# A relational graph layer: every second adjacency chunk is loaded in quadrant form and turned by VectorE

## The chip, the cores and the metric

The kernel runs on one core of a Trainium2 chip. The metric is the device time of one execution in microseconds. The core has TensorE (PE), VectorE (DVE), ScalarE (ACT), GpSimd (POOL) and SyncE (SP), each with a queue of its own that is worked off in order; SP and ACT can issue DMA transfers from theirs. Waits are on semaphores.

## What is computed

For each of 8 batches there is x (1024 x 128, float32) and an adjacency matrix of 1024 x 1024 int32. Its entries are 0 or, as drawn here, 1; the kernel checks on the way that nothing else occurs and has a second, general path for that case, which does not run with these inputs.

```python
masks = (relation[None] == rel_ids[:, None, None, None]).astype(x.dtype)   # rel_ids 1..4
h = jnp.einsum('rbnm,bmd->rbnd', masks, x)
y = jnp.einsum('rbnd,rdo->bno', h, weight) + bias
out = layernorm(x + y)                                                     # over the last axis
```

## The kernel before, in words

**Chunks.** The adjacency of a batch is cut into 4 chunks of 256 rows (1 MB of int32 each), 32 chunks in all, u = 0 to 31. SBUF holds them as 128 partitions of 2048 words, in a ring of 8 slots (`NADJ`). Partition p of chunk c holds rows 8p + 2c and 8p + 2c + 1. A half (`hf`, 0 to 15) is two chunks, so half a batch.

**The way of a chunk.** SP issues the load (`load_adj`, L152). ACT converts the int32 words to fp8 bytes (`convert_chunk`, L171, `mask`, ring of 4). The product needs the columns of the adjacency on the partitions, so PE transposes the mask, four bytes taken together as one float32 word, in four transposes of 128 x 128 words into a PSUM bank (`turn_words`, L178, `tp_ps`). DVE copies that bank to SBUF (`evacuate`, L182, `maskT`, ring of 6) and ORs the words into `seen` (L451), from which the check for other values is made at the end (`find_others`).

**Products.** x is split into three bf16 parts (`x_sb`'s upper halves, `x_rest`'s upper halves, `x_fine`). Each half takes 3 x 8 matmuls of 512 columns (L194) into one bank of `h_ps`; ACT copies the bank (L386), PE multiplies by the weight (`project_half`, L201), DVE adds x + bias (`add_half`, L477), takes mean and variance (L207, L212, L216), POOL makes the scale and the shift, and DVE (L223) and ACT (L398) each normalise half of the rows. Outputs are stored by SP behind all loads.

**Order.** Each engine's program is written out by hand. On PE the half `hf` is

```python
for part in range(PARTS):
    last = part_products(part, b % NX, b % 2, slice(place, place + 2), bank_of(hf))
    if part == 0:
        turn(2 * hf + 2)
    if part == 1:
        project_half(hf - 1)
        turn(2 * hf + 3)
```

and ACT's turn for it is `copy_half(hf)`, `convert(2 * hf + 5)`, `finish_half(hf - 1)`, `convert(2 * hf + 6)`. Chunks 0 and 1 come as four pieces with shorter products; the first and the last half are cut in quarters. SP's queue in the start is: pieces of chunk 0, x of batch 0, pieces of chunk 1, chunks 2 and 3, x 1, chunk 4, bias, weight, chunk 5, x 2, chunks 6 to 9, x 3, and so on; a chunk from 8 on waits until the one eight back is converted.

## Time and profile before

| | us |
|---|---|
| median of 3 runs | 139.17 |
| lowest, highest | 138.47, 139.57 |
| the profiled execution | 138.68 |
| its span in the profile | 136.9 |
| PE busy | 124.1 |
| DVE busy | 85.8 |
| ACT busy | 83.0 |
| POOL busy | 69.2 |
| read from HBM, written | 37.88 MB, 4.19 MB |

The span is what the profile shows between the first and the last instruction; the execution's own time is 1.8 us longer. Busy times are those of one engine added up, and say nothing yet about which one the others wait for.

### The profile page before, as it was taken

What the parts mean: (1) busy time and instruction counts of PE and PEld (TensorE: products, weight loads), DVE (VectorE), ACT (ScalarE), POOL (GpSimd) and SP (SyncE); (2) the same over time, 40 slices, a digit from 0 to 9 for tenths busy, and PEclk for the clock granted to TensorE, in tenths of its full rate; (3) what the DMA queues carried; (4) which work ended last, traced back from release to release, by engine and by line L of the source; (5) the groups of instructions that cost most, each with busy time, mean ns of one, the idle gap of its engine ahead of it and who ended that gap; (6) DMA issues with size and microseconds to landing.
All of it is one profiled execution on the core that took longest, in us unless ns stands there. A gap on an engine that the chain in (4) does not pass through costs nothing.

```text
span 136.9 us, 2235 instructions
## 1 busy us (share of the span) xinstructions
PE 124.1 (91%) x727; PEld 77.2 (56%) x727; DVE 85.8 (63%) x270; ACT 83.0 (61%) x85; POOL 69.2 (51%) x79
## 2 busy tenths in 40 slices
PE   5986799489999999999999999999999999997920
PEld 2355688346564747465565656565656474666810
DVE  1185213765758494958677675757585939488851
ACT  3655753379785848484848586777758484513040
POOL 3000019975295709680786259553957195405440
PEclk9999999999999999999999999999999999999985
DMA  4999969999999999999999999999913000300422
GB/s 125 415 427 418 427 230 419 421 426 414 426 426 406 423 421 421 420 423 417 412 419 424 414 424 424 424 412 414 382 59 158 0 0 0 153 0 0 160 77 84
DMA packets 7789, 42.24 MB, mean 309 GB/s; under 512 B 864, under 2 KB 1376, under 8 KB 3936
## 3 DMA queue, kind: packets, MB, share of 16 engines
q1 hardware_dynamic: 7776, 42.08, 75.3%
q8 instruction: 7, 0.11, 0.3%
q14 instruction: 6, 0.05, 0.1%
HBM read 37.88 MB, written 4.19 MB: 307 GB/s over the span
## 4 chain that ended last, share of the span: by engine, by line
PE 73%; DMA 15%; SPq 4%; ACT 2%; DVE 1%; issue 1%; POOL 1%
PE h_ps L194 54%; DMA adj_sb<-in_adj_dram 15%; PE y_ps L201 10%; PE tp_ps L178 9%; ACT mask L171 1%; SPq L152 1%; SPq L258 1%; SPq L155 1%; POOL scale L219 1%; ACT h_sb L392 0%; DVE out_sb L223 0%; DVE stats L207 0%; ACT out_sb L398 0%; SPq L270 0%; SPq L269 0%
## 5 line engine op out<-in xcount | busy, mean ns | idle before, releaser
L171 ACT ACTIVATE mask<-adj_sb 128x2048 fp8e4<-128x2048 int32 x30 | 57.2, 1906 | 9.0 <-DMA adj_sb<-in_adj_dram 9.0
L194 PE MATMUL h_ps<-maskT,x_sb 128*128 128x512 fp8e4 (+1 forms) x152 | 32.0, 352 | 3.5 <-DVE maskT L182 2.5
L194 PE MATMUL h_ps<-maskT,x_fine 128*128 128x512 fp8e4 (+1 forms) x152 | 32.0, 352 | 0.4 <-DVE x_fine L164 0.4
L194 PE MATMUL h_ps<-maskT,x_rest 128*128 128x512 fp8e4 (+1 forms) x152 | 32.0, 352 | 0.1
L182 DVE COPY maskT<-tp_ps 128x512 uint32<-128x512 uint32 x30 | 20.6, 686 | 17.2 <-PE tp_ps L178 17.2
L167 POOL TENSOR_TENSOR x_bias<-x_sb,bias_sb 128x1024 f32<-128x1024 f32 x8 | 19.0, 2380 | 18.2 <-DMA bias_sb<-in_L_gnn_bias_dram 18.2
L194 PEld LDWEIGHTS h_ps<-maskT,x_sb 128*128 128x128 bf16 x152 | 14.3, 96 | 18.7 <-DVE maskT L182 2.9
L335 POOL TENSOR_SCALAR minus_mean<-mean_var 128x4 f32<-128x4 f32 (+1 forms) x16 | 3.1, 193 | 41.7 <-issue 22.9
L477 DVE TENSOR_TENSOR total<-y_ps,x_bias 128x512 f32<-128x512 f32 (+1 forms) x17 | 11.2, 660 | 20.2 <-issue 19.2
L386 ACT COPY h_sb<-h_ps 128x512 f32<-128x512 f32 x13 | 7.6, 585 | 23.4 <-issue 23.4
L178 PE MATMUL tp_ps<-identity,mask 128*128 128x128 f32 x128 | 21.1, 286 | 0.7 <-ACT mask L171 0.4
L178 PEld LDWEIGHTS tp_ps<-identity,mask 128*128 128x128 f32 x128 | 18.8, 204 | 4.9 <-ACT mask L171 1.2
L194 PEld LDWEIGHTS h_ps<-maskT,x_fine 128*128 128x128 bf16 x152 | 14.7, 97 | 11.8 <-DVE x_fine L164 0.7
L194 PEld LDWEIGHTS h_ps<-maskT,x_rest 128*128 128x128 bf16 x152 | 14.7, 97 | 11.3 <-DVE x_rest L161 0.3
L451 DVE TENSOR_TENSOR seen<-seen,tp_ps 128x512 uint32<-128x512 uint32 x30 | 20.3, 677 | 0.0
L201 PEld LDWEIGHTS y_ps<-w_sb,h_sb 128*128 128x128 f32 x128 | 16.6, 191 | 3.7 <-ACT h_sb L392 1.4
L219 POOL TENSOR_TENSOR scale<-var_eps,power 128x4 f32<-128x4 f32 (+1 forms) x17 | 17.8, 1046 | 1.7 <-DVE var_eps L216 1.7
L201 PE MATMUL y_ps<-w_sb,h_sb 128*128 128x128 f32 x128 | 17.3, 277 | 1.2 <-ACT h_sb L392 1.2
L398 ACT ACTIVATE out_sb<-total,shift,scale 128x128 f32<-128x128 f32 x31 | 13.6, 486 | 7.8 <-POOL shift L340 7.8
L207 DVE BATCH_NORM_STATS2 stats<-total 128x6 f32<-128x128 f32 x64 | 13.9, 279 | 0.2
L164 POOL TENSOR_TENSOR x_fine<-x_rest 128x1024 bf16<-128x1024 f32 x7 | 13.3, 1893 | 0.1
L161 POOL TENSOR_TENSOR x_rest<-x_sb 128x1024 f32<-128x1024 f32 x7 | 13.3, 1895 | 0.0
(28 smaller groups left out, 46.4 us busy)
## 6 DMA issues: line engine op xcount, KB each, us to landing
adj_sb<-in_adj_dram SPq DMA_DIRECT2D x30, 1024.0 KB, 17.6
x_sb<-in_x_dram SPq DMA_DIRECT2D x8, 512.0 KB, 17.9
out_dram<-out_sb SPq DMA_DIRECT2D x7, 512.0 KB, 7.7
adj_sb<-in_adj_dram SPq DMA_DIRECT2D x4, 512.0 KB, 5.2
out_dram<-out_sb SPq DMA_DIRECT2D x1, 256.0 KB, 2.0
out_dram<-out_sb SPq DMA_DIRECT2D x2, 128.0 KB, 1.8
bias_sb<-in_L_gnn_bias_dram SPq DMA_DIRECT2D x1, 64.0 KB, 14.8
w_sb<-in_L_gnn_weight_dram SPq DMA_DIRECT2D x1, 64.0 KB, 14.6
```

The lines of the kernel that those rows point to most:

```text
L161: eng.tensor_tensor(x_rest[:, slot], x_sb[:, x_slot], upper(x_sb[:, x_slot]), ALU.subtract).then_inc(done, 1)
L164: eng.tensor_tensor(x_fine[:, slot], x_rest[:, slot], upper(x_rest[:, slot]), ALU.subtract).then_inc(done, 1)
L167: nc.gpsimd.tensor_tensor(x_bias[:, slot], x_sb[:, x_slot], bias_sb[:, :].unsqueeze(1).to_broadcast([P, TILES, D]), ALU.add).then_inc(done, 1)
L171: nc.scalar.activation(mask[:, slot % NMASK], adj_sb[:, slot % NADJ], ACT.Copy, saturate=False).then_inc(done, 1)
L178: last = nc.tensor.transpose(tp_ps[:, bank, place:place + P], words[:, o, j], identity[:, :])
L182: nc.vector.tensor_copy(maskT[:, place].rearrange("k j o p e -> k (j o p e)").bitcast(u32), tp_ps[:, bank].bitcast(u32)).then_inc(done, 1)
L194: last = nc.tensor.matmul(h_ps[:, bank, 0:n], x_t, m_t, start=(part == 0 and t == 0), stop=(part == PARTS - 1 and t == TILES - 1))
L201: last = nc.tensor.matmul(y[:, n, :], h_of(r)[:, s], w_sb[:, r, :], start=(r == 0), stop=(r == relations - 1))
L207: last = nc.vector.bn_stats(stats[:, slot, s, :], total[:, place, s, :])
L219: nc.gpsimd.tensor_tensor(scale[:, slot, tiles], var_eps[:, slot, tiles], power[:, tiles], ALU.pow).then_inc(done, by)
L398: last = nc.scalar.activation(out_sb[:, b, s, :], total[:, b % NTOTAL, s, :], ACT.Identity, bias=shift[:, b % 2, s:s + 1], scale=scale[:, ...
L451: nc.vector.tensor_tensor(seen[:, :], seen[:, :], tp_ps[:, tp_bank(u)].bitcast(u32), ALU.bitwise_or).then_inc(collected, 1)
```

## The change

Chunks with u > 4 and u odd (5, 7, ..., 31, fourteen of them; `by_blocks`) are no longer loaded by SP. ACT issues them, each as four transfers (`load_quadrant`), at places written into its program: chunk 5 before the conversion of chunk 2, chunk 7 behind it, 9 and 11 behind those of chunks 3 and 4, 13 and 15 behind those of 6 and 8, and then 2 * hf + 13 at the end of the turn for each half. Quadrant q fills partitions 32q to 32q + 31 with the columns 256q to 256q + 255 of the chunk's 256 rows, in 256 runs of 256 words (1 KB). After the conversion, one transposition of 32 x 32 blocks on DVE (`turn_blocks`) brings `maskT` into the form that the product wants; no transpose on PE and no copy from PSUM is made for these chunks, and DVE's OR reads `mask` in place of the bank.

Since the rows of a quadrant are every fourth row, the rows of a chunk are numbered anew for all chunks: partition p of a row-wise chunk c holds rows 8p + c and 8p + 4 + c, two runs of 4 KB in place of one of 8 KB. The projection of a `by_blocks` chunk reads `h_sb` with a stride of two (`rows_of`), and `total` and `out_sb` are addressed through `tile_of` and `by_chunk`. The last batch's stores are cut by chunk (`store_chunks`), in runs of 1 KB and 512 B. The general path's store and sums follow the new order. The core of the diff:

```diff
     NBANK = 3
     NTP = 3
     PIECED = 2
+    Q = 4
+    S = P // Q
     NY = 2
     BANK = 512
     EPS = 1e-5
...
     x_p = x.rearrange("b (p t) d -> b p (t d)", p=P)
     out_p = out.rearrange("b (p t) d -> b p (t d)", p=P)
-    adj_p = adj.rearrange("b (p c o) m -> b c p (o m)", p=P, c=CH)
+    out_t = out.rearrange("b (p o c) d -> b p o (c d)", p=P, c=CH)
+    adj_p = adj.rearrange("b (p o c) m -> b c p o m", p=P, c=CH)
+    adj_q = adj.rearrange("b (g r c) (q m) -> b c q r g m", r=S, c=CH, q=Q)
 
     ctx = ExitStack()
     with ctx:
...
             return values.bitcast(bf16).rearrange("p t (d two) -> p t two d", two=2)[:, :, 1, :]
 
         def load_adj(eng, b, ch, slot, done):
-            eng.dma_start(adj_sb[:, slot], adj_p[b, ch]).then_inc(done, 16)
+            eng.dma_start(adj_sb[:, slot].rearrange("p (o m) -> p o m", o=O), adj_p[b, ch]).then_inc(done, 16)
+
+        def load_quadrant(eng, b, ch, slot, q, done):
+            eng.dma_start(adj_sb[q * S:(q + 1) * S, slot].rearrange("r (g m) -> r g m", m=N // Q),
+                          adj_q[b, ch, q]).then_inc(done, 16)
 
         def load_x(eng, b, slot, done):
             eng.dma_start(flat(x_sb[:, slot]), x_p[b]).then_inc(done, 16)
 
-        def store(eng, b, place, tiles, done):
-            eng.dma_start(out_p[b][:, tiles.start * D:tiles.stop * D], flat(out_sb[:, place, tiles])).then_inc(done, 16)
+        def by_chunk(tiles):
+            return tiles.rearrange("p (o c) d -> p c o d", o=O)
+
+        def tile_of(s):
+            return s // O + CH * (s % O)
+
+        def store(eng, b, place, done):
+            eng.dma_start(out_p[b], flat(out_sb[:, place])).then_inc(done, 16)
+
+        def store_chunks(eng, b, place, chunks, done):
+            eng.dma_start(out_t[b][:, :, chunks.start * D:chunks.stop * D],
+                          out_sb[:, place].rearrange("p (o c) d -> p o (c d)", o=O)[:, :, chunks.start * D:chunks.stop * D]
+                          ).then_inc(done, 16)
 
         def take_rest(eng, x_slot, slot, done):
             eng.tensor_tensor(x_rest[:, slot], x_sb[:, x_slot], upper(x_sb[:, x_slot]), ALU.subtract).then_inc(done, 1)
...
         def evacuate(bank, place, done):
             nc.vector.tensor_copy(maskT[:, place].rearrange("k j o p e -> k (j o p e)").bitcast(u32),
                                   tp_ps[:, bank].bitcast(u32)).then_inc(done, 1)
+
+        def turn_blocks(slot, place, done):
+            blocks = mask[:, slot].bitcast(u32).rearrange("r (g s j) -> r j g s", s=S, j=J)
+            nc.vector.transpose(maskT[:, place].rearrange("k j o p e -> k (j o p e)").bitcast(u32), blocks).then_inc(done, 1)
 
         def evacuate_tile(bank, place, o, done):
             nc.vector.tensor_copy(maskT[:, place, :, o].rearrange("k j p e -> k j (p e)").bitcast(u32),
...
                                         start=(part == 0 and t == 0), stop=(part == PARTS - 1 and t == TILES - 1))
             return last
 
-        def project(h_of, y, relations, tiles, done, by):
-            for n, s in enumerate(range(tiles.start, tiles.stop)):
-                for r in range(relations):
-                    last = nc.tensor.matmul(y[:, n, :], h_of(r)[:, s], w_sb[:, r, :],
-                                            start=(r == 0), stop=(r == relations - 1))
-            last.then_inc(done, by)
+        def project(rows, y, r, relations, n):
+            return nc.tensor.matmul(y[:, n, :], rows, w_sb[:, r, :], start=(r == 0), stop=(r == relations - 1))
+
+        def rows_of(h, u, c, o):
+            if by_blocks(u):
+                return h[:, c * O:(c + 1) * O].rearrange("d t p -> d (t p)").rearrange("d (p o) -> d o p", o=O)[:, o]
+            return h[:, c * O + o]
 
         def measure_rows(slot, place, tiles, done, by):
             for s in range(tiles.start, tiles.stop):
-                last = nc.vector.bn_stats(stats[:, slot, s, :], total[:, place, s, :])
+                last = nc.vector.bn_stats(stats[:, slot, s, :], total[:, place, tile_of(s), :])
             last.then_inc(done, by)
 
         def aggregate_rows(slot, tiles, done, by):
...
         def normalize(b, slot, place, tiles, done, by):
             for s in tiles:
-                last = nc.vector.tensor_scalar(out_sb[:, b, s, :], total[:, place, s, :], mean_var[:, slot, s, 0:1],
-                                               scale[:, slot, s:s + 1], ALU.subtract, ALU.mult)
+                last = nc.vector.tensor_scalar(out_sb[:, b, tile_of(s), :], total[:, place, tile_of(s), :],
+                                               mean_var[:, slot, s, 0:1], scale[:, slot, s:s + 1], ALU.subtract, ALU.mult)
             last.then_inc(done, by)
 
         def bank_of(hf, c=0):
             return (hf + 2 if hf > 1 else 2 * hf) % NBANK if c == 0 else (bank_of(hf) + c) % NBANK
 
+        def by_blocks(u):
+            return u > CH and u % 2 == 1
+
+        def by_rows_before(u):
+            return sum(not by_blocks(v) for v in range(PIECED, u))
+
         def tp_bank(u, o=0):
-            return (PIECED * O + u - PIECED if u >= PIECED else O * u + o) % NTP
+            return (PIECED * O + by_rows_before(u) if u >= PIECED else O * u + o) % NTP
+
+        def last_in_bank(u):
+            turned_before = PIECED * O + by_rows_before(u) - NTP
+            if turned_before < PIECED * O:
+                return turned_before // O
+            return [v for v in range(PIECED, u) if not by_blocks(v)][turned_before - PIECED * O]
+
+        def landed(u):
+            return sum(16 * (Q if by_blocks(v) else 1) for v in range(PIECED, u + 1) if v % NADJ == u % NADJ)
 
         def gathered(u):
             return u + 1 + PIECED * (O - 1) if u >= PIECED else O * u + 1
...
                 load_x(sp, b, b % NX, x_loaded[b % NX])
 
             def load_piece(u, o):
-                sp.dma_start(adj_sb[:, u, o * N:(o + 1) * N],
-                             adj_p[0, u][:, o * N:(o + 1) * N]).then_inc(piece_loaded[O * u + o], 16)
+                sp.dma_start(adj_sb[:, u, o * N:(o + 1) * N], adj_p[0, u][:, o]).then_inc(piece_loaded[O * u + o], 16)
 
             load_piece(0, 0)
             load_piece(0, 1)
...
             for b in range(LAST):
                 sp.wait_ge(normed, CH * (b + 1))
                 sp.wait_ge(act_normed, CH * (b + 1))
-                store(sp, b, b, ALL, stored)
+                store(sp, b, b, stored)
             sp.wait_ge(normed, CH * LAST + 2)
             sp.wait_ge(act_normed, CH * LAST + 2)
-            store(sp, LAST, LAST, HALF[0], stored)
+            store_chunks(sp, LAST, LAST, slice(0, 2), stored)
             for c in range(2):
                 sp.wait_ge(normed, CH * LAST + 3 + c)
                 sp.wait_ge(act_normed, CH * LAST + 3)
-                store(sp, LAST, LAST, QUARTER[2 + c], stored)
+                store_chunks(sp, LAST, LAST, slice(2 + c, 3 + c), stored)
 
             sp.wait_ge(flag_ready, 1)
             again = sp.value_load(flag[0:1, 0:1], min_val=0, max_val=P)
...
         @block.scalar
         def _(act):
             def convert(u):
-                act.wait_ge(adj_loaded[u % NADJ], 16 * (u // NADJ + (1 if u % NADJ >= PIECED else 0)))
+                act.wait_ge(adj_loaded[u % NADJ], landed(u))
                 if u >= NMASK:
-                    wait_chunk(act, piece_turned, turned, u - NMASK)
+                    free_mask(u - NMASK)
                 convert_chunk(u, masked)
+
+            def free_mask(u):
+                if by_blocks(u):
+                    act.wait_ge(evacuated, u - PIECED + 1)
+                    act.wait_ge(collected, gathered(u) + 1)
+                elif u >= PIECED:
+                    act.wait_ge(turned, by_rows_before(u) + 1)
+                else:
+                    act.wait_ge(piece_turned, O * (u + 1))
+
+            def load_blocks(u):
+                if u >= NADJ:
+                    wait_chunk(act, piece_masked, masked, u - NADJ)
+                for q in (0, 2, 1, 3):
+                    load_quadrant(act, u // CH, u % CH, u % NADJ, q, adj_loaded[u % NADJ])
 
             def copy_half(hf):
                 act.wait_ge(multiplied, 2 * (hf + 1))
...
                     act.wait_ge(piece_loaded[O * u + o], 16)
                     nc.scalar.activation(mask[:, u, o * N:(o + 1) * N], adj_sb[:, u, o * N:(o + 1) * N],
                                          ACT.Copy, saturate=False).then_inc(piece_masked, 1)
+            load_blocks(5)
             convert(2)
+            load_blocks(7)
             copy_quarter(0, 0)
             convert(3)
+            load_blocks(9)
             copy_quarter(0, 1)
             convert(4)
+            load_blocks(11)
             convert(5)
             copy_quarter(1, 0)
             copy_quarter(1, 1)
             convert(6)
+            load_blocks(13)
             convert(7)
             finish_half(0)
             convert(8)
+            load_blocks(15)
             for hf in range(2, HALVES - 1):
                 copy_half(hf)
                 if 2 * hf + 5 < UNITS:
...
                 finish_half(hf - 1)
                 if 2 * hf + 6 < UNITS:
                     convert(2 * hf + 6)
+                if 2 * hf + 13 < UNITS:
+                    load_blocks(2 * hf + 13)
             copy_quarter(HALVES - 1, 0)
             copy_quarter(HALVES - 1, 1)
             finish_half(HALVES - 2)
...
                 evacuate_tile(tp_bank(u, o), u, o, piece_evacuated)
 
             def empty_bank(u):
-                dve.wait_ge(turned, u - PIECED + 1)
+                dve.wait_ge(turned, by_rows_before(u) + 1)
                 if u >= NMT:
                     dve.wait_ge(multiplied, 2 * ((u - NMT) // 2 + 1))
                 evacuate(tp_bank(u), u % NMT, evacuated)
                 collect(u)
 
-            def add(b, y, c_slice, hf, count, by):
+            def turn_chunk(u):
+                dve.wait_ge(masked, u - PIECED + 1)
+                if u >= NMT:
+                    dve.wait_ge(multiplied, 2 * ((u - NMT) // 2 + 1))
+                turn_blocks(u % NMASK, u % NMT, evacuated)
+                dve.wait_ge(collected, gathered(u))
+                nc.vector.tensor_tensor(seen[:, :], seen[:, :], mask[:, u % NMASK].bitcast(u32),
+                                        ALU.bitwise_or).then_inc(collected, 1)
+
+            def ready(u):
+                if by_blocks(u):
+                    turn_chunk(u)
+                else:
+                    empty_bank(u)
+
+            def add(b, y, chunks, hf, count, by):
                 dve.wait_ge(projected, count)
                 dve.wait_ge(biased, b + 1)
                 if hf % 2 == 0 and b >= NTOTAL:
                     dve.wait_ge(act_normed, CH * (b - NTOTAL + 1))
-                tiles = slice(HT * (hf % 2) + O * c_slice.start, HT * (hf % 2) + O * c_slice.stop)
-                nc.vector.tensor_tensor(total[:, b % NTOTAL, tiles], y, x_bias[:, b % 2, tiles], ALU.add).then_inc(added, by)
+                cs = slice(2 * (hf % 2) + chunks.start, 2 * (hf % 2) + chunks.stop)
+                nc.vector.tensor_tensor(by_chunk(total[:, b % NTOTAL])[:, cs], y.rearrange("p (c o) d -> p c o d", o=O),
+                                        by_chunk(x_bias[:, b % 2])[:, cs], ALU.add).then_inc(added, by)
 
             def measure(b, tiles, count, by):
                 dve.wait_ge(added, count)
...
             collect_piece(1, 0)
             collect_piece(1, 1)
             for hf in range(HALVES - 1):
-                empty_bank(2 * hf + 2)
+                ready(2 * hf + 2)
                 if hf >= 1:
                     add_half(hf - 1)
-                empty_bank(2 * hf + 3)
+                ready(2 * hf + 3)
                 if hf >= 1:
                     measure_half(hf - 1)
                 if hf >= 2:
...
                     pe.wait_ge(x_split, b + 1)
 
             def turn(u):
-                before = u - NTP if u >= PIECED + NTP else (u + 1 - PIECED) // O
+                if by_blocks(u):
+                    return
                 pe.wait_ge(masked, u - PIECED + 1)
-                wait_chunk(pe, piece_evacuated, evacuated, before)
-                pe.wait_ge(collected, gathered(before + 1))
+                wait_chunk(pe, piece_evacuated, evacuated, last_in_bank(u))
+                pe.wait_ge(collected, gathered(last_in_bank(u) + 1))
                 turn_words(u % NMASK, tp_bank(u), range(O), turned)
 
             def project_half(hf):
                 pe.wait_ge(h_copied, 2 * (hf + 1))
                 if hf >= 2:
                     pe.wait_ge(added, 2 * (hf - 1))
-                project(lambda r: h_sb[:, hf % 2], y_ps[:, hf % 2], 1, HALF[0], projected, 2)
+                for s in range(HT):
+                    last = project(rows_of(h_sb[:, hf % 2], 2 * hf + s // O, s // O, s % O), y_ps[:, hf % 2], 0, 1, s)
+                last.then_inc(projected, 2)
 
             def project_quarter(hf, c):
                 pe.wait_ge(h_copied, 2 * hf + c + 1)
                 pe.wait_ge(added, 2 * (hf - 1 + c))
-                project(lambda r: h_sb[:, hf % 2], y_ps[:, (1 + c) % NY], 1, QUARTER[c], projected, 1)
+                for o in range(O):
+                    last = project(rows_of(h_sb[:, hf % 2], 2 * hf + c, c, o), y_ps[:, (1 + c) % NY], 0, 1, o)
+                last.then_inc(projected, 1)
 
             def products_half(hf):
                 b = hf // 2
```

## Rows read from the trace of the kernel before

**Rows 1.** The page, sections 1 and 2: engine totals and 40 slices.

```profile
PE 124.1 (91%) x727; PEld 77.2 (56%) x727; DVE 85.8 (63%) x270; ACT 83.0 (61%) x85; POOL 69.2 (51%) x79
...
DMA  4999969999999999999999999999913000300422
```

**Rows 2.** Chain that ended last: start us, length us, what.

```profile
7.13 20.49 DMA adj_sb<-in_adj_dram
...
37.12 0.47 PE tp_ps L178 x4
...
37.59 1.80 PE h_ps L194 x8
...
39.39 0.89 PE y_ps L201 x8
...
40.76 3.61 PE h_ps L194 x16
```

**Rows 3.** Groups of instructions by form: count, busy us, mean ns, idle before.

```profile
L194 PEld LDWEIGHTS h_ps<-maskT,x_fine 128*128 128x128 bf16 x152 | 14.7, 97 | 11.8 <-DVE x_fine L164 0.7
...
L194 PEld LDWEIGHTS h_ps<-maskT,x_sb 128*128 128x128 bf16 x152 | 14.3, 96 | 18.7 <-DVE maskT L182 2.9 <-DVE maskT L186 1.7
...
L182 DVE COPY maskT<-tp_ps 128x512 uint32<-128x512 uint32 x30 | 20.6, 686 | 17.2 <-PE tp_ps L178 17.2
...
L161 DVE TENSOR_TENSOR x_rest<-x_sb 128x1024 f32<-128x1024 f32 x1 | 1.2, 1216 | 0.0
```

**Rows 4.** Windows view, 36 to 44 us.

```profile
36.00:44.00 8.00, 8.00 (x45) 4.61 (x44) 5.65 (x23) 5.83 (x6) 5.70 (x6) 1.00 1.01 417
```

**Rows 5.** Timeline of the start, ACT and PE: start us, length us, what.

```profile
9.51 1.06 ACT L408 ACTIVATE mask<-adj_sb 128x1024 fp8e4<-128x1024 int32 x1 [0.21 <-DMA adj_sb<-in_adj_dram]
...
11.99 1.91 ACT L171 ACTIVATE mask<-adj_sb 128x2048 fp8e4<-128x2048 int32 x1 [1.43 <-DMA adj_sb<-in_adj_dram]
...
18.23 1.91 ACT L171 ACTIVATE mask<-adj_sb 128x2048 fp8e4<-128x2048 int32 x1 [1.57 <-DMA adj_sb<-in_adj_dram]
...
22.74 1.91 ACT L171 ACTIVATE mask<-adj_sb 128x2048 fp8e4<-128x2048 int32 x1 [2.60 <-DMA adj_sb<-in_adj_dram]
...
27.18 1.97 PE L194 MATMUL h_ps<-maskT,x_sb 128*128 128x512 fp8e4 x8 [1.73 <-DVE maskT L182]
...
27.64 1.91 ACT L171 ACTIVATE mask<-adj_sb 128x2048 fp8e4<-128x2048 int32 x1 [2.45 <-DMA adj_sb<-in_adj_dram]
...
30.13 1.91 ACT L171 ACTIVATE mask<-adj_sb 128x2048 fp8e4<-128x2048 int32 x1 [0.58 <-DMA adj_sb<-in_adj_dram]
```

**Rows 6.** Timeline of SP's queue: start us, length us of the issue.

```profile
7.64 1.52 SPq L152 DMA_DIRECT2D adj_sb<-in_adj_dram  x1
...
9.21 2.13 SPq L152 DMA_DIRECT2D adj_sb<-in_adj_dram  x1
...
11.38 0.43 SPq L152 DMA_DIRECT2D adj_sb<-in_adj_dram  x1
...
11.86 3.32 SPq L155 DMA_DIRECT2D x_sb<-in_x_dram  x1
...
29.57 0.33 SPq L152 DMA_DIRECT2D adj_sb<-in_adj_dram  x1
```

**Rows 7.** DMA view, 134.1 to 134.4 us: packets, MB, share.

```profile
DMA packets 76, 0.06 MB, mean 205 GB/s; under 512 B 16, under 2 KB 76, under 8 KB 76
...
q1 hardware_dynamic: 76, 0.06, 62.2%
```

**Rows 8.** DMA view, 18.2 to 19.2 us.

```profile
q1 hardware_dynamic: 115, 0.08, 45.1%
```

**Rows 9.** Timeline of one half, all engines.

```profile
75.25 1.90 ACT L171 ACTIVATE mask<-adj_sb 128x2048 fp8e4<-128x2048 int32 x1
...
76.61 0.69 DVE L477 TENSOR_TENSOR total<-y_ps,x_bias 128x512 f32<-128x512 f32 x1 [1.46 <-issue]
...
77.22 0.68 DVE L182 COPY maskT<-tp_ps 128x512 uint32<-128x512 uint32 x1
...
78.41 1.67 PEld L194 LDWEIGHTS h_ps<-maskT,x_sb 128*128 128x128 bf16 x8
...
78.88 0.58 ACT L386 COPY h_sb<-h_ps 128x512 f32<-128x512 f32 x1 [1.73 <-issue]
```

**Rows 10.** Timeline of ACT, the last conversion.

```profile
115.59 1.92 ACT L171 ACTIVATE mask<-adj_sb 128x2048 fp8e4<-128x2048 int32 x1
```

More of the change, by code:

```diff
@@ L298, in _ @@
                     sp.wait_ge(g_normed, b + 1)
[L299 removed]
+                    store(sp, b, 0, g_stored)
                 sp.wait_ge(g_stored, 16 * (B + 1))
@@ L707, in _ @@
                     for half in range(2):
-                        project(lambda r: h_all[:, r], y_ps[:, half], R, HALF[half], g_projected, 1)
+                        for s in range(HT):
+                            for r in range(R):
+                                last = project(h_all[:, r, HT * half + s], y_ps[:, half], r, R, s)
+                        last.then_inc(g_projected, 1)
             pe.end_ifs()
```

9 lines of the change are left out of this document (6 added, 3 removed).

## The prediction

> **What bounds the kernel now.** Read the page's totals first, then the chain of waits in order of time, then the windows. In the totals PE is at 91% and the DMA slices stay full until about 97 us [rows 1], so two resources look like the bound, and the chain tells where each is. Up to 27.6 us it runs along the loads [rows 2]: ACT sits idle before each conversion until that chunk has landed (11.99, 18.23, 22.74, 27.64, 30.13 us for chunks 2, 4, 5, 6, 7) [rows 5]. From about 30 us to 125 us it is PE alone, in a fixed pattern per half batch: first part 1.80, transposes of the next even chunk 0.47, second part 1.80, projection 0.89, transposes of the next odd chunk 0.47, third part 1.80 us; the row of 3.61 is a third part and the next first part together [rows 2]. The period is 3 x 1.80 + 2 x 0.47 + 0.89 = 7.24 us (exact pieces 7.24 or 7.25). PE has no idle time in 36 to 44 us, at granted clock 1.00 of full speed, while DMA moves 417 GB/s [rows 4]: it is running ahead, held back by nothing that PE waits for. Half 3 starts at 37.12 - 1.80 = 35.3 us [rows 2]; half 2 at 27.18 us [rows 5].
>
> **The change part by part.** The profiled execution took 138.68 us (span 136.9); the median of the three runs, 139.17, is 0.5 above, which I add at the end.
>
> *Transposes removed from PE.* Chunks 5, 7, ..., 31 are 14 chunks, each four transposes, 0.47 us in the chain [rows 2]. Chunk 5's are done before 27.18, after which PE waits for data, so they buy nothing; chunk 7's lie in half 2, whose length the start decides. From half 3 to half 14 there are 12: 12 x 0.47 = 5.6 us off, and the period becomes 6.77.
>
> *VectorE.* The copy from PSUM (0.686 us [rows 3]) becomes a 32x32 transposition of as many words between SBUF tiles; the trace has none. Below it is bounded by the copy it replaces, above by 1.22 us, the slowest SBUF operation of DVE here, over twice the elements [rows 3]. I take the copy's, as the count is the same. It now follows the add directly: add from 76.61, copy from 77.22 to 77.90, next half's weights at 78.41 [rows 9]. PE comes there 0.47 sooner, at 77.94, so the cover is about 0.04 us, and the copy itself was waiting on nothing but the add. I charge 0; at 1.22 it costs 0.5 x 12 = 6 us. The collect then reads SBUF instead of PSUM, same count; measure, variances and finish are queued behind it. The new wait (masked instead of turned) is met early: the odd chunk's conversion follows the copy of h at the start of the half [rows 9]. ACT's conversion of the chunk four later now waits for this transposition and collect; they are over most of a half before.
>
> *Loads.* Every even chunk now comes as two rows of 4 KB a partition, not one of 8: same rate, since x comes in 4 KB rows in the full slices too. Odd ones become four transfers of 256 packets of 1 KB. Price of such a packet: in the last stores, 60 packets of 1 KB and 16 tiny ones take 0.622 x 16 x 0.3 = 2.99 us of engine time, 49 ns each [rows 7]. So a chunk is 1024 x 49 / 16 = 3.1 us, where 417 GB/s gives 2.5 [rows 4]. The other neighbour is the stretch of bias and weights, 103 packets of 512 B in 1 us [rows 8], which would make 9.9 us of a chunk; half of those read one and the same 512 B, so I take 3.1 and keep the other end. Weights with stride two load as fast as dense ones (96 against 97 ns, [rows 3]), so the interleaved projection costs nothing; and the two last stores, in 512 B pieces, have 8 packets more an engine, at most 8 x 49 ns = 0.4 us, which I leave in the range.
>
> *Issues on ACT's queue: the term that decides.* Each costs 0.33 to 0.43 us on SP [rows 6]; four make 1.3 to 1.7. Late in the kernel they stand behind a conversion of 1.90 us, with 1.73 us idle after it [rows 9], so they are covered (cover gone: ACT's cycle of 5.5 us, waits included, plus 1.7 is 7.2, above 6.77). The wait in front, for the mask of the chunk eight back, is long met then. Queued behind are the copy of h and the next conversions, for which PE waits.
> In the start it is otherwise. SP's issues of chunks 7 and 8 and of x 3 took 1.52, 2.13 and 3.32 us with nothing to wait for [rows 6]. That is a full queue, and its limit is not a number of transfers: chunk 8's issue ended at 11.34, though nothing landed between 9.51 (second piece of chunk 1) and 11.99 (chunk 2) [rows 5, 6]. At that time 2, 3, x1, 4, bias, weights, 5, x2, 6, 7, 8 were out, 11 transfers of 8 packets for each of 16 engines, less the moved 0.73 of chunk 2: some 82. I take 84 as what ACT's queue holds too. A quadrant is 16 packets an engine, so it holds five; chunk 7's last two must wait, and ACT with them.
> How fast it drains depends on how two queues share the engines, which no row shows. Bounds: equal bytes, or one transfer in turn. I take turns, as the queues' unit in every row is the transfer or packet, not the byte. The Trainium skill (DMA: Bandwidth & Descriptors, "Queues, rings and completion order") says engines go round the queues by packets, typically 9 to 17 descriptors; by that the turns hold, by its absence the equal bytes of the rival below.
> Stepping it: SP's list after 9.6 us is the rest of 2 (to 12.0), 3, x1, 4, bias, weights, x2, 6, 8, x3, 10 at 2.5 a chunk, 1.25 an x, and 0.5 for each small one; after each one quadrant of 0.78. The quadrants then end at 12.8, 16.1, 18.1, 21.4, 22.7, 23.9, 26.0, 29.2, 32.5, 34.6, 37.8. The n-th can be issued once 16n - 84 packets an engine are done: n = 8 at 2.75 quadrants, 17.9 us; n = 12 at 6.75, 25.8 us; n = 16 at 10.75, 37.6 us. In ACT's order chunk 3's conversion stands behind n = 8, chunk 4's behind n = 12 (18.23 before), chunk 5's behind n = 16 (22.74 before). Chunk 5's mask ends at 37.6 + 1.9 = 39.5, half 2 starts at 40.2 (27.18 before), half 3 at 40.2 + 6.8 = 47.0 (35.3 before): 11.7 us late.
> Sum: 138.7 + 11.7 - 5.6 = 144.8 us, as a median 145.3.
>
> **The rivals.**
> *B, the faster side: ACT is hardly held.* If ACT's queue takes all quadrants, or the streams share well, the start moves by between 0 and 4.9 us. The upper end: with equal bytes, SP's 3.4 MB to the end of chunk 4 share with 3.1 MB of 5, 7, 9: 6.5 / 0.417 = 15.6 us after 9.6, chunk 4 at 25.2, and by the same sum chunk 6 at 33.3; half 3 starts at 40.2. Time 133.1 to 138.0, middle 135.5, as a median 136. For it: steady issues are short, and SP's long ones fall in the start alone [rows 6]. Against: the start is just where ACT must issue four chunks.
> *C, slower: the loads become the bound.* From chunk 7 (30.1 [rows 5]) to the last conversion (115.6 - 5.6 = 110.0 [rows 10]) lie 80 us for 12 even and 12 odd chunks and 5 of x: an odd one may take (80 - 30 - 6.3) / 12 = 3.65 us. Above that each 0.1 costs 1.2 us; should a quadrant run at half of 417 GB/s (5.0 us) the time is 133 + 16 = 149. For it: short packets and 32 partitions; against: 3.1 by rows 7. The Trainium skill (SBUF — State Buffer, "Door 1: The DMA port swizzle") has 32 partitions reach half the ports, 189 GB/s against 328 for 1 MiB; no row here shows a transfer to 32 partitions, and by it C holds.
> *D, no gain: DVE or ACT takes PE's place* after a good start: a transposition near 1.2 us, or issues that hold ACT (7.2 a half). Then 138 to 140.
> That the transposes stay on PE is excluded by the code.
>
> **How the numbers follow.** A 0.43, B 0.31, C 0.12, D 0.14. A change of under 1% (1.4 us) can't be told from none here. Slower: A and C, 0.55. Faster: B less its end near 138, with a bit of D, 0.30. Same: 0.15. The range goes from the lower part of B, 134, to 151, which holds A with up to 6 us more (chunk 7's conversion may be held again behind chunk 13's issues) and half of C; left out are B's best case, 0.05, and the tops of A and C, 0.1.
>
> **What would show it.** Right: issues on ACT's queue of several us between 12 and 38 us; ACT idle with data landed; half 2's first 512-column products near 40 us; then a period of 6.8. B: issues of 0.4 us each, half 2 before 31. C: ACT waiting for DMA after 50 us, DMA slices full to the end. D: period above 7, PE waiting for DVE's transposition or ACT's copy. My number is wrong if ACT's queue holds 16 quadrants, or if a blocked issue lets later ACT work pass.

## The result, and the profile after

The changed kernel takes 166.67 us, the median of 4 runs (165.90 to 168.21), against 139.37 for the kernel before on the same chip (138.47 to 140.01): a ratio of 1.198, interval 1.186 to 1.210. The profiled execution took 167.4 us, with a span of 165.6. In three experiments (quadrants on SP's queue from chunk 5 and from chunk 25, and narrow transfers with long packets) most executions fell into a slower state of the chip, so for these the fastest stands beside the median, no ratio is given, and their traces are of a slow one.

The page of the changed kernel, totals and 40 slices, with the chain's shares:

```profile
PE 125.1 (76%) x671; PEld 73.9 (45%) x671; DVE 90.0 (54%) x270; ACT 82.0 (50%) x85; POOL 69.1 (42%) x79
...
PE   6978700029395799599849999999957999999650
...
PEclk9999975556999999999975999999996999999996
DMA  5999999999999999999999999999999910030303
GB/s 175 418 416 349 320 303 337 336 337 230 244 337 339 240 226 305 338 292 225 314 337 277 230 315 339 279 271 296 318 402 354 229 78 0 0 131 0 128 31 104
...
ACTq 33%; PE 25%; issue 14%; ACT 13%; DMA 5%; DVE 3%; POOL 2%; SPq 1%; POOLq 0%; DVEq 0%
```

Beside [rows 1] read two things. PE stands idle in slices 6 to 8 (20.7 to 33.1 us). And DMA is full until about 132 us, at rates that mostly swing between 225 and 340 GB/s, where before it was full until 97 us at some 420. A busy share alone would call both "full". ACT's queue, which was not in the chain of [rows 2], now holds a third of it.

ACT in the start (the queue's own time is ACTq; a line without it is a compute instruction; `<-issue` is idle time for which the profile shows no releaser, here ACT standing in an issue):

```profile
11.96 6.10 ACTq L162 DMA_DIRECT2D adj_sb<-in_adj_dram  x4
...
18.37 1.91 ACT L193 ACTIVATE mask<-adj_sb 128x2048 fp8e4<-128x2048 int32 x1
18.59 17.06 ACTq L162 DMA_DIRECT2D adj_sb<-in_adj_dram  x3
...
35.96 1.91 ACT L193 ACTIVATE mask<-adj_sb 128x2048 fp8e4<-128x2048 int32 x1
36.44 4.14 ACTq L162 DMA_DIRECT2D adj_sb<-in_adj_dram  x3
40.68 1.91 ACT L193 ACTIVATE mask<-adj_sb 128x2048 fp8e4<-128x2048 int32 x1 [2.81 <-issue]
...
42.97 6.84 ACTq L162 DMA_DIRECT2D adj_sb<-in_adj_dram  x1
...
52.15 1.91 ACT L193 ACTIVATE mask<-adj_sb 128x2048 fp8e4<-128x2048 int32 x1 [7.21 <-issue]
```

These answer to [rows 5]. The conversions of chunks 3, 4, 5 and 7 start at 18.4, 36.0, 40.7 and 52.2 us; each stands behind issues that take 4.7 (chunk 5) to 17.5 us (chunk 4). On PE the halves 2 and 3 begin with these rows, and two late halves with the last two:

```profile
45.02 1.99 PE L220 MATMUL h_ps<-maskT,x_sb 128*128 128x512 fp8e4 x8 [2.60 <-DVE maskT L209]
...
54.85 1.98 PE L220 MATMUL h_ps<-maskT,x_sb 128*128 128x512 fp8e4 x8 [2.88 <-DVE maskT L209]
...
136.43 1.97 PE L220 MATMUL h_ps<-maskT,x_sb 128*128 128x512 fp8e4 x8
...
143.22 1.97 PE L220 MATMUL h_ps<-maskT,x_sb 128*128 128x512 fp8e4 x8
```

The period there is 143.22 - 136.43 = 6.79 us, so the saving on PE is there in full. Where the time is: half 3 starts at 54.85 against 35.3 [rows 2], 19.5 us late; the last products end at 157.45 + 1.07 = 158.5, so 13 halves take 103.7, or 7.97 each, where they took 94.8. That is 19.5 + 8.9 = 28.4 of the 28.7 us between the two profiled executions.

The 7.97 is a mean, and no half is like it. Most of the halves from half 3 on take 6.8 to 7.2 us, also while the loads still run; three take 9.2, 12.7 and 11.5 us (those that start at 61.79, 77.77 and 118.14), and these three hold 13.0 us of delay. What they have in common (timeline of ACT, PE's waits from 54 us on, and the window behind the longest of them):

```profile
60.30 7.08 ACTq L162 DMA_DIRECT2D adj_sb<-in_adj_dram  x2
...
76.35 8.10 ACTq L162 DMA_DIRECT2D adj_sb<-in_adj_dram  x2
84.57 0.59 ACT L444 COPY h_sb<-h_ps 128x512 f32<-128x512 f32 x1 [6.53 <-issue]
...
118.77 5.68 ACTq L162 DMA_DIRECT2D adj_sb<-in_adj_dram  x3
...
PE y_ps L225 <- ACT h_sb L444: 8.1, 3, 3.2
...
84.00:91.00 7.00, 5.79 (x18) 3.20 (x19) 3.48 (x14) 5.18 (x6) 0.35 (x2) 0.54 1.06 305
```

Each time ACT stands in issues of 5.7 to 8.1 us, the copy of h stands behind them, and PE's projection waits for the copy, 8.1 us in all; the other 4.9 us are PE at a lower granted clock behind two of these waits. ACT waits for no load after chunk 2, and the last conversion starts at 143.95 us, some 11 us after the loads are over. So to its end the changed kernel is bound not by data that come late but by ACT being held, again and again, in the issues of slow transfers.

The rate, in the windows view (busy time of PE, PEld, DVE, ACT, POOL with counts, granted clock, DMA share, GB/s):

```profile
28.00:35.00 7.00, 0.00 (x0) 0.00 (x0) 0.00 (x0) 0.00 (x0) 2.45 (x2) 0.50 1.05 337
56.00:59.00 3.00, 3.00 (x16) 1.60 (x15) 2.50 (x10) 2.60 (x3) 1.86 (x4) 1.00 1.13 227
```

The DMA view of the same two stretches shows whose packets they are:

```profile
q1 hardware_dynamic: 493, 1.89, 82.9%
q10 hardware_dynamic: 491, 0.47, 21.7%
...
DMA packets 706, 0.68 MB, mean 227 GB/s; under 512 B 40, under 2 KB 706, under 8 KB 706
...
q10 hardware_dynamic: 706, 0.68, 112.9%
```

From 28 to 35 us the two queues move 493 and 491 packets, one for one: 1 MB by rows with one quadrant (1.31 MB) in 1.31 / 0.337 = 3.9 us. From 56 to 59 us ACT's queue is alone, the engines are busier than ever (share 1.13), and 227 GB/s pass: 262 KB / 0.227 = 1.15 us a quadrant, 4.6 us a chunk. So a pair of chunks costs 3.9 + 3 x 1.15 = 7.35 us, and with half of an x, which took 1.25 us before, 7.97. The stream as a whole, 301 GB/s from 25 to 128 us, gives 2.36 MB / 0.301 = 7.8 us a pair. That 7.97 is also the mean of the 13 halves is in part chance: the last four of them run when the loads are over or nearly so.

### The profile page after: what moved, and what is told of

Its sections match the earlier page's. It is cut to its first block, busy times and chain, and to the rows that moved or that the text cites. A ratio compares the mean times of both kernels' runs of the same rounds, so it can differ in the third digit from the quotient of the medians.

```text
span 165.6 us, 2151 instructions
## 1 busy us (share of the span) xinstructions
PE 125.1 (76%) x671; PEld 73.9 (45%) x671; DVE 90.0 (54%) x270; ACT 82.0 (50%) x85; POOL 69.1 (42%) x79
## 4 chain that ended last, share of the span: by engine, by line
ACTq 33%; PE 25%; issue 14%; ACT 13%; DMA 5%; DVE 3%; POOL 2%; SPq 1%; POOLq 0%; DVEq 0%
ACTq L162 33%; PE h_ps L220 19%; ACT mask L193 8%; DMA adj_sb<-in_adj_dram 5%; PE y_ps L225 5%; ACT out_sb L456 3%; POOL scale L246 2%; PE tp_ps L200 1%; ACT h_sb L444 1%; SPq L302 1%; ACT h_sb L450 1%; DVE stats L234 1%; DVE mean_var L239 0%; DVE seen L543 0%; DVE out_sb L250 0%
## 5 line engine op out<-in xcount | busy, mean ns | idle before, releaser
L193 ACT ACTIVATE mask<-adj_sb 128x2048 fp8e4<-128x2048 int32 x30 | 57.2, 1906 | 11.5 <-issue 10.0
L225 PE MATMUL y_ps<-w_sb,h_sb 128*128 128x128 f32 x128 | 20.4, 308 | 24.9 <-ACT h_sb L450 16.7
L220 PE MATMUL h_ps<-maskT,x_sb 128*128 128x512 fp8e4 (+1 forms) x152 | 33.4, 363 | 7.3 <-DVE maskT L209 5.5
L220 PE MATMUL h_ps<-maskT,x_fine 128*128 128x512 fp8e4 (+1 forms) x152 | 34.7, 372 | 0.4 <-DVE x_fine L186 0.4
L225 PEld LDWEIGHTS y_ps<-w_sb,h_sb 128*128 128x128 f32 x128 | 18.7, 215 | 28.6 <-issue 15.3
L204 DVE COPY maskT<-tp_ps 128x512 uint32<-128x512 uint32 x16 | 11.0, 689 | 31.1 <-PE tp_ps L200 31.0
L220 PEld LDWEIGHTS h_ps<-maskT,x_sb 128*128 128x128 bf16 x152 | 14.8, 100 | 23.6 <-DVE maskT L209 7.6
L220 PEld LDWEIGHTS h_ps<-maskT,x_fine 128*128 128x128 bf16 x152 | 15.3, 101 | 13.6 <-issue 3.1
L220 PEld LDWEIGHTS h_ps<-maskT,x_rest 128*128 128x128 bf16 x152 | 14.9, 99 | 11.5 <-DVE x_rest L183 0.3
L543 DVE TENSOR_TENSOR seen<-seen,mask 128x512 uint32<-128x512 uint32 x14 | 13.6, 973 | 0.0
L450 ACT COPY h_sb<-h_ps 128x256 f32<-128x256 f32 x6 | 2.1, 366 | 23.2 <-issue 19.6
L200 PEld LDWEIGHTS tp_ps<-identity,mask 128*128 128x128 f32 x72 | 11.0, 203 | 4.7 <-ACT mask L193 1.1
## 6 DMA issues: line engine op xcount, KB each, us to landing
out_dram<-out_sb SPq DMA_DIRECT2D x7, 512.0 KB, 10.9
```

The lines of the kernel that those rows point to most:

```text
L193: nc.scalar.activation(mask[:, slot % NMASK], adj_sb[:, slot % NADJ], ACT.Copy, saturate=False).then_inc(done, 1)
L200: last = nc.tensor.transpose(tp_ps[:, bank, place:place + P], words[:, o, j], identity[:, :])
L220: last = nc.tensor.matmul(h_ps[:, bank, 0:n], x_t, m_t, start=(part == 0 and t == 0), stop=(part == PARTS - 1 and t == TILES - 1))
L225: return nc.tensor.matmul(y[:, n, :], rows, w_sb[:, r, :], start=(r == 0), stop=(r == relations - 1))
L543: nc.vector.tensor_tensor(seen[:, :], seen[:, :], mask[:, u % NMASK].bitcast(u32), ALU.bitwise_or).then_inc(collected, 1)
```

## The experiments

Two theories stood against each other. **H** (held): the loss is ACT, held by its own full queue in the start; the quadrants cost 3.1 us a chunk, as predicted. **P** (partitions): a transfer into 32 partitions runs at about half the rate, whoever issues it. Each run is told with the time of the kernel before on the same chip, or its ratio to it.

### Who issues, and how many partitions: four kernels in a square

**Quadrants by SP.** ACT issues nothing.

```diff
             def load_unit(u):
-                if by_blocks(u):
-                    return
...
-                load_adj(sp, u // CH, u % CH, u % NADJ, adj_loaded[u % NADJ])
+                if by_blocks(u):
+                    for q in (0, 2, 1, 3):
+                        load_quadrant(sp, u // CH, u % CH, u % NADJ, q, adj_loaded[u % NADJ])
+                else:
+                    load_adj(sp, u // CH, u % CH, u % NADJ, adj_loaded[u % NADJ])
...
             def load_blocks(u):
+                return
```

> The quadrant transfers are issued by SP, in place of the row-wise load of the same chunk, so ACT issues no DMA; all else as in the changed kernel. Theory H (the time comes from ACT being held by its full queue, the quadrants themselves cost 3.1 us a chunk): nothing is left of the loss, PE bounds at 6.8 us a half, 133 to 135 us. Theory P (transfers into 32 partitions run at about half the rate, the changed kernel shows one ending about every 1.15 us, so 4.6 us a chunk against 2.5): the loads end near 97 + 14 x 2.1 = 126 us and behind them come a conversion, a transposition, a quarter's products and the tail, 142 to 146 us.

Measured: 168.0 us, median of 4 (165.21 to 175.29), against 138.93. H's number is refuted: with ACT free, half 2 starts at 29.93 us, and the time is as bad as before. P names the mechanism, but its number, 142 to 146, is missed by 20 us: its price was too low. Here it is the data that come late, as they do not in the changed kernel. ACT's waits, and DMA in 60 to 100 us:

```profile
ACT mask L193 <- DMA adj_sb<-in_adj_dram: 71.7, 30, 6.6
...
DMA packets 5687, 9.40 MB, mean 235 GB/s; under 512 B 349, under 2 KB 4415, under 8 KB 5684
```

**Rows by SP, turned by VectorE.** The change without its loads.

```diff
         def landed(u):
-            return sum(16 * (Q if by_blocks(v) else 1) for v in range(PIECED, u + 1) if v % NADJ == u % NADJ)
+            return sum(16 for v in range(PIECED, u + 1) if v % NADJ == u % NADJ)
...
             def load_unit(u):
-                if by_blocks(u):
-                    return
...
             def load_blocks(u):
+                return
```

> Odd chunks from the sixth on are loaded row-wise by SP like the others (4 KB runs, 128 partitions), but still turned by DVE and not by PE; the blocks of the mask so end in wrong places and the products are of other data. This is the compute part of the change alone. Both theories: 133 to 134 us (12 x 0.47 us less than before). If DVE's transposition were the trouble: above 137.

Measured: 134.49 us, ratio 0.964 (0.957 to 0.971), within half a microsecond of what both theories said. VectorE's transposition and the rest of the program keep up.

**Same sizes, all partitions.** Four transfers of 256 KB a chunk in packets of 1 KB as before, but each into 128 partitions; once with ACT issuing (first), once with SP (second, with the edit of the first experiment too).

```diff
-            eng.dma_start(adj_sb[q * S:(q + 1) * S, slot].rearrange("r (g m) -> r g m", m=N // Q),
-                          adj_q[b, ch, q]).then_inc(done, 16)
+            cols = slice(q * (N // Q), (q + 1) * (N // Q))
+            eng.dma_start(adj_sb[:, slot].rearrange("p (o m) -> p o m", o=O)[:, :, cols],
+                          adj_p[b, ch][:, :, cols]).then_inc(done, 16)
```

> ACT issues four transfers at the same places as in the changed kernel, each of 256 packets of 1 KB, but each over all 128 partitions (a quarter of the columns of every row), so number, size and issue of the packets stay and only the spread over partitions goes; the data are not those of the product. Theory H: still late, ACT held in the start as reckoned for 3.1 us a chunk, 143 to 148 us. Theory P: near 134 to 137. Both together: H's figure, clearly under the changed kernel's 166.7.

> The same transfers over 128 partitions with 1 KB packets, issued by SP: neither ACT held nor 32 partitions. If small packets alone cost 3.1 us a chunk: loads end near 105 us, 133 to 135 us. If 1 KB packets are what makes the quadrants slow (and not the partitions), as e1 by theory P: 142 to 146 us.

Measured: 147.94 us by ACT, ratio 1.063 (1.056 to 1.070); 134.24 us by SP, 0.964 (0.956 to 0.972). The same bytes in the same 1 KB pieces of HBM move in SP's kernel, 30 to 95 us, at

```profile
DMA packets 14930, 24.67 MB, mean 380 GB/s; under 512 B 915, under 2 KB 11591, under 8 KB 14922
```

so 1 KB packets are cheap, and what is left as the cause of the halved rate is the 32 partitions. ACT's kernel shows the other cause by itself:

```profile
19.76 13.20 ACTq L163 DMA_DIRECT2D adj_sb<-in_adj_dram  x3
...
33.27 1.91 ACT L194 ACTIVATE mask<-adj_sb 128x2048 fp8e4<-128x2048 int32 x1
...
42.39 1.98 PE L221 MATMUL h_ps<-maskT,x_sb 128*128 128x512 fp8e4 x8 [2.60 <-DVE maskT L210]
...
49.18 1.98 PE L221 MATMUL h_ps<-maskT,x_sb 128*128 128x512 fp8e4 x8
```

The square: wide by SP 134.2, wide by ACT 147.9, narrow by SP 165.2 to 168.0, narrow by ACT 166.7. Each cause alone makes the change a loss. They don't add up in this square. Narrow by SP and narrow by ACT are alike in time, not in kind: by SP conversions wait for data, by ACT they wait for ACT; and in SP's kernel the row-wise transfers behind the quadrants are slowed as well (below). With wide transfers ACT is held in the start alone, and from half 3 on the period is 6.8; with narrow ones it is held until the last issue.

### Is it the packet or the partitions?

Still 32 partitions, by SP, but 8 KB from each in one piece of HBM.

```diff
+    adj_l = adj.rearrange("b (c q r o) m -> b c q r (o m)", c=CH, q=Q, r=S)
...
-            eng.dma_start(adj_sb[q * S:(q + 1) * S, slot].rearrange("r (g m) -> r g m", m=N // Q),
-                          adj_q[b, ch, q]).then_inc(done, 16)
+            eng.dma_start(adj_sb[q * S:(q + 1) * S, slot],
+                          adj_l[b, ch, q]).then_inc(done, 16)
```

> Four transfers a chunk into 32 partitions each, issued by SP as in e1, but with runs of 8 KB (32 packets a transfer instead of 256), of other rows than the product needs. Theory P in the form 'few partitions are slow, whatever the packet': like e1, 155 to 170 us, about 1.2 us a transfer. In the form 'short packets into few partitions are slow': 133 to 140 us.

Measured: 169.98 us, median of 3 (165.62 to 171.80), against 138.59. In 60 to 100 us:

```profile
DMA packets 2325, 10.15 MB, mean 254 GB/s; under 512 B 366, under 2 KB 366, under 8 KB 1809
```

Less than half as many packets for more bytes, and nearly the rate of the 1 KB quadrants (235). The packet is not the cause.

### Quadrants only late in the kernel

If the start were the trouble, later quadrants would be free. ACT's queue, from chunk 17:

```diff
-            return u > CH and u % 2 == 1
+            return u > 2 * NADJ and u % 2 == 1
...
             def load_blocks(u):
+                if not by_blocks(u):
+                    return
```

> The quadrant form on ACT's queue as in the changed kernel, but from chunk 17 on (eight chunks), so that the start is as before and ACT's queue is empty when it begins. Theory H in its narrow form (ACT is held in the start alone): 8 x 0.47 = 3.8 us gained, 135 us. Theory P: loads end near 97 + 8 x 3.2 = 123 us, and ACT is held whenever its queue is full: 145 to 150 us.

Measured: 152.20 us, ratio 1.097 (1.091 to 1.104), just above the 145 to 150 of theory P. The third batch of issues holds ACT for 12.7 us, and PE is busy for 2.54 of the 10 us from 60; another holds it for 9.3 us from 70.9.

```profile
54.43 12.74 ACTq L162 DMA_DIRECT2D adj_sb<-in_adj_dram  x3
```

H as a matter of the start falls too; ACT held wherever its queue is full, which theory P's text had in it, stands.

SP's queue, the last four and the last six odd chunks (`u > 24`, `u > 20`, with the edit of the first experiment):

> The quadrant form for chunks 25, 27, 29 and 31 alone, issued by SP; all others row-wise and turned by PE. From e1 a chunk in quadrants costs about 3.4 us more than a row-wise one, so the loads end near 97 + 4 x 3.4 = 111 us, about when the last conversion needs them. Theory P with this price: 4 x 0.47 = 1.9 us gained, 137.0 us; if the price is higher than that, no gain, 138 to 141.

> As e7 with chunks 21 to 31, six of them. The loads end near 97 + 6 x 3.4 = 117 us, some 5 to 7 us too late for PE, against 2.8 us of transposes saved: 140 to 143 us. If the lead of the loads hides more than reckoned: 136.4.

Measured: four give 139.67 us, median of 6 (136.69 to 143.88), against 138.59: unclear. Six give 149.94, ratio 1.074 (1.067 to 1.081), worse than the 140 to 143 expected. So the lead that the loads have over PE pays for a few quadrants and no more. In the six-chunk kernel conversions wait 29.5 us for DMA in all, where they waited 9.0 in the kernel before; 100 to 115 us:

```profile
100.00:115.00 15.00, 12.34 (x59) 6.56 (x58) 7.71 (x24) 6.95 (x9) 3.27 (x4) 0.88 1.08 228
```

### What fills ACT's queue, and who waits behind it

Packets or transfers? Four transfers a chunk by ACT into 128 partitions with 2 KB packets: 8 packets for each engine, not 16.

```diff
+    adj_w = adj.rearrange("b (p c o) m -> b c p (o m)", p=P, c=CH)
...
-            eng.dma_start(adj_sb[q * S:(q + 1) * S, slot].rearrange("r (g m) -> r g m", m=N // Q),
-                          adj_q[b, ch, q]).then_inc(done, 16)
+            part = slice(q * (O * N // Q), (q + 1) * (O * N // Q))
+            eng.dma_start(adj_sb[:, slot, part], adj_w[b, ch][:, part]).then_inc(done, 16)
```

> As e3 (ACT issues four transfers a chunk over 128 partitions), but each has 128 packets of 2 KB, 8 for an engine in place of 16; contents are row-wise, so the products are of other data. If ACT's queue is limited in packets (about 84 an engine): four chunks come to 128, the last issue of the start ends once 44 are done, near 24 us instead of 38, and the time is 134 to 137 us. If it is limited in transfers (five): as e3, 146 to 149 us.

Measured: 139.66 us, ratio 1.007 (1.004 to 1.011).

```profile
20.98 3.87 ACTq L164 DMA_DIRECT2D adj_sb<-in_adj_dram  x4
24.95 1.91 ACT L194 ACTIVATE mask<-adj_sb 128x2048 fp8e4<-128x2048 int32 x1 [2.07 <-issue]
...
24.86 1.99 PE L226 MATMUL y_ps<-w_sb,h_sb 128*128 128x128 f32 x8 [4.20 <-DMA w_sb<-in_L_gnn_weight_dram]
```

The same 16 transfers are now out at 24.85 us, near the 24 of a limit in packets and far from the 38 of one in transfers. How sharp is the limit? When a blocked issue ends, count the packets issued and take off those that the DMA view has as moved in ACT's queue: in the changed kernel 12 x 16 - 1750 / 16 = 83 an engine at 35.65 us, but 8 x 16 - 350 / 16 = 106 at 18.06; here 16 x 8 - 916 / 16 = 71. In transfers that is five to nine. So 84 is an estimate of a limit that lies between 71 and 106, and a part of the match with 24 is luck.

The time missed its 134 to 137 for another reason, which the last row shows: PE waits 4.2 us for the weights, which stand in SP's queue. One transfer a chunk by ACT leaves only this:

```diff
         def landed(u):
-            return sum(16 * (Q if by_blocks(v) else 1) for v in range(PIECED, u + 1) if v % NADJ == u % NADJ)
+            return sum(16 for v in range(PIECED, u + 1) if v % NADJ == u % NADJ)
...
-                for q in (0, 2, 1, 3):
-                    load_quadrant(act, u // CH, u % CH, u % NADJ, q, adj_loaded[u % NADJ])
+                load_adj(act, u // CH, u % CH, u % NADJ, adj_loaded[u % NADJ])
```

> ACT issues each odd chunk as one row-wise transfer over 128 partitions (16 packets of 4 KB an engine), at the same places; turned by DVE, so the products are of other data. Nothing should hold ACT (four chunks are 64 packets an engine). If the two queues take turns transfer by transfer, chunks 5, 7, 9 and 11 move ahead of 4 and 6: chunk 4 lands near 23 us (18.2 before), chunk 6 near 33 (27.6), 136 to 140 us. If the queue were served in order of issue: 133 to 135.

Measured: 142.01 us, ratio 1.026 (1.020 to 1.032), above the 136 to 140 expected. ACT's issues take 0.55 us each and hold nothing, and still:

```profile
24.26 1.91 ACT L193 ACTIVATE mask<-adj_sb 128x2048 fp8e4<-128x2048 int32 x1 [6.74 <-DMA adj_sb<-in_adj_dram]
...
27.38 2.08 PE L225 MATMUL y_ps<-w_sb,h_sb 128*128 128x128 f32 x8 [6.86 <-DMA w_sb<-in_L_gnn_weight_dram]
```

Chunk 4 is converted at 24.3 (18.23 before) because chunks 5, 7 and 9 take turns with it in another queue: with two queues, early prefetch delays what is urgent.

### As many quadrants as the lead pays for

Chunks 27, 29 and 31 by SP (`u > 26`):

> The quadrant form for chunks 27, 29 and 31 alone, by SP: loads end near 97 + 3 x 4.5 = 111 us, in time, and 3 x 0.47 = 1.4 us are saved: 137.5 us, at the edge of what can be measured. If quadrants late in the stream hurt as in e7: 138 to 140.

Measured: 140.55 us, ratio 1.010 (1.006 to 1.014), slower than either number. Yet in its profiled execution (139.60) PE's last products end at 128.9 us, 1.2 us sooner than before (130.1). SP's waits at the end of the program say where it went; the kernel before has 0.2 us in this place:

```profile
SPq L54 <- PEq L54: 2.5, 1, 2.5
```

PE's program is shorter by the transposes. The next kernel gives it 33 instructions that wait for a signal long there, and changes nothing else:

```diff
             keep_warm(9)
+            for _ in range(33):
+                pe.wait_ge(warm_set, 1)
```

> As e10 (chunks 27, 29, 31 in quadrants, issued by SP), with 33 waits that are met at once put into PE's program behind its first nine matmuls, so that this program is about as long again as that of the kernel before. In e10 PE's last products end 1.2 us earlier than in the kernel before, but after the last store has landed SP still waits 2.5 us for PE to reach the end of the program (0.2 us before). If that is where PE's code for the end lies, padding brings it back to about 0.2: 137.5 us, 1% faster than before. If not: 139.5 to 140.5 as e10.

Measured: 137.14 us, median of 6, against 138.58: ratio 0.988 (0.983 to 0.994), the one version that computes the layer and clearly beats both kernels. Four executions took 137.0 to 137.2 us and two, the profiled one among them, 138.5 and 138.7. Its wait there, and that of the kernels with four and with six late quadrant chunks:

```profile
SPq L54 <- PEq L54: 0.2, 1, 0.2
...
SPq L54 <- PEq L54: 2.8, 1, 2.8
...
SPq L54 <- PEq L54: 2.6, 1, 2.6
```

That 33 instructions in PE's program take the wait of 2.5 us away is shown. That a shorter program has the longer wait is not: it is 0.2 us with 727 PE instructions on the page (the kernel before), 2.8, 2.5 and 2.6 with 711, 715 and 703 (four, three, six late chunks), and 0.2 again with 695 (from chunk 17) and with 671 (the changed kernel and all the rest). What in the program decides it stays open. The kernels with four and six late chunks carry it too, so by estimate some 2.5 us of their times are not the quadrants' own.

## Why the prediction was wrong

The forecast was slower, 145.3 us; 166.67 lies above the range's end of 151.

**The step that failed** is "So a chunk is 1024 x 49 / 16 = 3.1 us", the price of a chunk in quadrants. It took the price of a 1 KB packet from stores that read 128 partitions [rows 7] and used it for loads into 32. Wide transfers with such packets do bear it out: of the 24.67 MB at 380 GB/s some 10.9 MB went in 1 KB packets, and with the rest at 417 GB/s that leaves 3.1 us for 1 MB of them, an estimate. So the packet was priced rightly; the partitions were the term left out. Measured: 4.6 us with the queue alone, 7.35 a pair in turns, so an odd chunk takes 7.35 - 2.5 = 4.85 us, above the break-even of 3.65 that the text had worked out itself. The kernel with wide transfers by ACT is the changed kernel with only this term taken out (its data are then other ones), and it takes 147.94 us: 2.6 from the forecast and inside the range.

**What hangs on it** is "so they are covered", said of ACT's issues late in the kernel. Four were to take 1.3 to 1.7 us behind a conversion. With transfers that drain slowly ACT's queue is full there too, and issues of 5.7 to 8.1 us held the copy of h in three halves. C had the slow loads, but with the wrong effect: by its own sum an odd chunk of 4.85 us gives 133 + 12 x (4.85 - 3.65) = 147 us, and its sign, "ACT waiting for DMA after 50 us", doesn't appear in the changed kernel. The held ACT and the slow loads stood as cases with chances of their own (A 0.43, C 0.12), so no forecast had one acting through the other. By parts, from the changed kernel's own trace: half 3 at 54.85 in place of 47.0 is +7.9, and 13 halves in 103.7 in place of 94.8 - 5.6 = 89.2 are +14.5; 144.8 + 22.4 = 167.2, and the profiled execution took 167.4. That closes because the parts are read from the same trace; it says where the time is, and the experiments say why.

**C** deserved more weight than 0.12. For it spoke "32 partitions"; against it only rows that had none. The rate measured, 227 GB/s against 417 [rows 4], is what separates them. The Trainium skill (SBUF — State Buffer, "Door 1: The DMA port swizzle") says that 32 partitions reach half the ports; this case's runs agree in kind, whatever the packet (235 and 254 GB/s in mixed stretches, 227 alone). C's own 149 us was low because it had a good start in it and no ACT that is held.

**A**, the held ACT, was right in mechanism and off in size. By itself (wide, by ACT) it puts half 2 at 42.4 and half 3 at 49.2, predicted 40.2 and 47.0; the time of that kernel is 147.94, predicted 145.3. In the changed kernel each quadrant also drains more slowly, and chunk 4's conversion comes at 36.0, predicted 25.8; half 2 at 45.0. The fear that chunk 7's conversion would be held again, put into the range at up to 6 us, came true: 52.15 us after 7.21 of idle time, and 2.9 us of PE's wait at half 3 stem from it. The limit in packets held in kind (24.85 us against 24), not in size: the eighth quadrant was out at 18.06 us against 17.9, but with 22 packets an engine moved and not 44, which is luck. The turns held (493 packets to 491). The Trainium skill (DMA: Bandwidth & Descriptors, "Queues, rings and completion order") has engines go round the queues by packets; the trace agrees in its counts (493 to 491), and shows nothing finer.

**The transposes** off PE were right: 6.79 us a half for a predicted 6.77, and -4.4 to -4.7 us in the two kernels that load fast. Of the predicted 5.6, a part goes to the start, where half 3 still begins near 35.7.

**VectorE's transposition** was taken at the copy's 0.69 us; it is 702 ns:

```profile
L209 DVE STREAM_TRANSPOSE maskT<-mask 128x512 uint32<-128x512 uint32 x14 | 9.8, 702 | 3.1 <-ACT mask L193 3.1
L543 DVE TENSOR_TENSOR seen<-seen,mask 128x512 uint32<-128x512 uint32 x14 | 13.6, 973 | 0.0
...
L517 DVE TENSOR_TENSOR seen<-seen,tp_ps 128x512 uint32<-128x512 uint32 x16 | 10.8, 676 | 0.0
```

**B** is refuted: the queue doesn't take all quadrants, and the issues hold ACT. **D** was not what decided: in the kernel with rows by SP the period is 6.8, with neither DVE nor ACT in PE's place.

**Not foreseen at all:** the clock. PE's 671 instructions take 125.1 us here and 118.9 in the wide kernel by SP. The granted clock is 0.50 in the idle stretch from 28 to 35 us, the 1.2 GHz level, and the slices show lower digits again (7, 5 and 6) where PE has waited for ACT. It is 0.54 from 84 to 91 us, behind a wait of 3.2 us: the projection takes 2.08 us there where it takes 1.08 elsewhere, and the third part 3.62 for 1.97. With the same behind the wait at 125 us this makes 4.9 us of the three long halves, so a good part of the 6.2 us lies on the path that sets the time.

**Still open:** why, in SP's queue, the row-wise transfers behind quadrants are slow. By the conversions, which all wait for DMA there, an even chunk with no x before it lands 3.6 to 4.7 us after the chunk before, where it takes 2.5 elsewhere, and a pair of chunks costs 9 to 10 us, its half of an x included. No run takes this apart.

## What to carry to other kernels

Before a load is split by partitions, look for a row that writes as few partitions: transfers into 32 ran at 227 GB/s here and the same bytes into 128 at up to 417 (380 in a mix with 1 KB packets), and no share of busy DMA shows it. Don't issue prefetch from an engine whose compute others wait for when its queue can fill (here at some 71 to 106 packets outstanding for each DMA engine): a blocked issue holds all that stands behind it, at any time in the kernel. And remember that a second queue takes turns with the first, so that early loads delay urgent ones. Rivals that rest on different resources can both come true, and one can act through the other: give the case of both its own time.

## What the runs showed of the hardware that was not expected

- VectorE's OR of two SBUF tiles has a mean of 973 ns against 676 with one operand in PSUM. One took 1.83 us beside a GpSimd add; the shortest took 0.65. It cost nothing on PE: with rows by SP its mean is 1180 ns, and the period is 6.8 us all the same. The rows, VectorE's and then GpSimd's:

```profile
61.47 1.83 DVE L543 TENSOR_TENSOR seen<-seen,mask 128x512 uint32<-128x512 uint32 x1
...
60.36 2.39 POOL L189 TENSOR_TENSOR x_bias<-x_sb,bias_sb 128x1024 f32<-128x1024 f32 x1
```

- The DMA share is highest, 1.13, where the rate is lowest (227 GB/s), and 1.01 at 417 [rows 4]: it must be read beside the rate.
- With 703 to 715 PE instructions SP waited 2.5 to 2.8 us for PE at the end of the program, with fewer or more 0.2; 33 instructions that do nothing took it away.
